# Keys of even tiles in the second place of the key buffer, and the first loads in another order

## The chip, the cores and the metric

The kernel runs on one core of one Trainium2 chip. The metric is the device time of one execution in microseconds (us). Engines: TensorE (PE, and PEld for its weight loads), VectorE (DVE), ScalarE (ACT), GpSimd (POOL), and SyncE (SP), which here only issues transfers.

## The reference, cut to what matters

The input is x of 4 batches x 1024 positions x 512. It goes through a layer norm, an attention with 16 heads of width 128, and a small product with quantised weights; all is added to x. Of the attention, these lines carry what the change touches:

```python
q  = apply_rope(rmsnorm(xn @ Wq + bq, qn_w), pos)
lk = apply_rope(rmsnorm(xn @ Wlk + blk, kn_w), pos)       # local keys
lv = xn @ Wlv + blv                                       # local values
sc = einsum(q, ck) * scale            # 256 compressed keys a batch, causal; the best 8 are kept
kw = concat([prev window of lk, this window of lk])       # windows of 128; none before the first
sl = where(band & (position exists), einsum(q, kw) * scale, NEG)
out = ((softmax(top 8) @ cv + softmax(sl) @ vw) * 0.5) @ Wo + bo
```

A query tile of 128 positions looks at its own 128 keys, at the 128 keys of the tile before it in the same batch, and at the compressed keys that are already complete. The first tile of a batch has no tile before it.

## The kernel before, in words

The work is cut into 256 units u = 64 * batch + 8 * pair + i: a pair of heads and a tile i of 128 positions. Unit u with u % 8 == 0 is the first tile of its batch for its pair of heads; there are 32 such units. The tiles of one pair follow each other, i = 0 to 7, so that the keys of the tile before are still in SBUF.

Every engine runs the same list of steps s, and in step s it works on several units at different stages: unit s is projected (`proj_qk`, lines 514 to 516), s-1 is transposed (`tr`, 540) and its values projected (`proj_v`, 530 to 532), s-2 is scored (`scores`, 561 to 563), s-3 has its weights transposed (`turn_p`, 571), s-4 meets the values (`values`, 586 and 589), s-5 goes through Wo (`out_proj`, 601 to 603). The order on each engine is written out by hand; engines wait for each other by semaphores. TensorE's order in a step is: first half of `proj_qk`, `scores`, `values`, second half of `proj_qk`, `tr`, `out_proj`, `turn_p`, `proj_v`.

Products that need more than the short float's precision are made of high and low halves in fp32r, three matmuls for one product. In `scores` these are q_hi by k_hi, q_hi by k_lo and q_lo by k_hi, for each of the two heads: six matmuls for a unit. The profile prints fp32r operands of matmuls as f32. Matmuls of plain f32 operands that are no transposes (`values`, and `entries` at line 631) appear as two records for one matmul in the code: `values` issues 384 matmuls at line 586, and the profile has 768.

The scored columns lie side by side in `qkh` and `qkl`, tiles of 5 x 128 columns for a head: 0 holds the queries, 1 and 2 hold local keys, 3 and 4 the compressed keys. Even tiles put their keys in place 1, odd tiles in place 2 (`qk_of`), so the other place still holds the tile before. `scores` takes n = 256 + C columns from place 1 on, with C = `width(u)` = 32 * (i + 1): 288 columns for a first tile, 512 for i = 7. A first tile uses only the 128 columns of its own keys (`nloc`) and the 32 compressed ones; place 2 is scored with it and not read. For the very first unit GpSimd fills place 2 with zeros (lines 1355 and 1356), and TensorE waits for that (semaphore `old`).

VectorE then adds a mask and takes the maximum (`mask_max`, 969), reading columns 0 to nloc of the scores; the block order of the weights in P follows the places, and `units_of` gives `values` the same order.

Before step 0 there are nine steps, from FIRST = -9 on, in which the eight tiles of batch 0 are normalised, transposed and split: VectorE `norm_stats` (1045 to 1049), GpSimd's power (1248), VectorE `normalise` (1056, 1060), TensorE `turn_x` (613) and `logits` (624), ScalarE `diagonal`, `hi_x`, `cast_x` (813, 791, 798), VectorE `group_max` and `lo_x` (1075, 1068). At the same time GpSimd splits the first weights (1303, 1305). In its order the split of chunk 0 stands ahead of the power of tile 1.

The first transfers stand in two queues. SP issues acc 0, acc 1, acc 2 (tiles of x), then chunks 0 and 1 of the weights, acc 3 and the rest. ACT issues `bcm`, `wcb`, `cst` (identity, masks, selectors: 352 KB) and two scalars into `isc`. VectorE waits for all of bcm, wcb and cst ahead of `normalise` of tile 0; TensorE waits for the same three before its first transpose.

Of the kernel before, what the change touches and what calls it, by code (L numbers as in the profile page):

```python
# [19 lines left out]
GONE = -3e38  # L20
# [5 lines left out]
C_ID, C_MK, C_MG, C_SEL, C_M32, C_N = 0, 128, 512, 640, 672, 704  # L26
# [4 lines left out]
FIRST, LAST = -AHEAD, NU + 6  # L31
# [9 lines left out]
    "kscale hi_qk p sq el es put_v hi_c wohi hi_x b8 ew put_et css hi_ck c8 "  # L41
    "lo_qk rs raw t1 krest add ngr mc m8 ttr mr nm lo_c acc wolo bs ba xv xn wl dg lo_x "
    "eg re wm init nb cke cm crest cadd cks lo_ck bl rsc isc wk tab rs0 "
# [4 lines left out]
).split()  # L48


def units_of(u):
    return [u] if u % 8 == 0 else [u, u - 1] if u % 2 == 0 else [u - 1, u]


def width(u):
    return 32 * (u % 8 + 1)


def nloc(u):
    return 128 if u % 8 == 0 else 256  # L60


def pblocks(u):
# [81 lines left out]
def build(nc, x, Wq, bq, Wcmp, bcmp, Wk, bk, Wv, bv, Wlk, blk, Wlv, blv, qnw, knw, Wo, bo,  # L145
# [3 lines left out]
    def sb(name, shape, dt=F32):  # L149
        return ctx.enter_context(nc.sbuf_tensor(name, shape, dt))  # L150
# [4 lines left out]
    with ctx:  # L155
        S = {name: ctx.enter_context(nc.semaphore("s_" + name)) for name in SIGNALS}
# [13 lines left out]
        qkh = sb("qkh", [128, 2, 5, 128], F32R)  # L170
        qkl = sb("qkl", [128, 2, 5, 128], F32R)
# [3 lines left out]
        t2 = sb("t2", [128, 2, 2, 64])  # L175
# [5 lines left out]
        P = sb("P", [128, 2, 2, 512])  # L181
        es = sb("es", [128, 2, 2, 256])
        rp = sb("rp", [128, 2, 256])
        e8 = sb("e8", [128, 2, 2, 8])
# [8 lines left out]
        q8 = sb("q8", [128, QR, 512], BF16)  # L193
# [3 lines left out]
        qb = sb("qb", [128, 512], BF16)  # L197
        qn = sb("qn", [128, 512], BF16)
# [6 lines left out]
        wcb = sb("wcb", [128, 512])  # L205
        bob = sb("bob", [128, 512])
        br = sb("br", [128, 2, 2, 2, 128])
        cst = sb("cst", [128, C_N])
# [16 lines left out]
        r4 = sb("r4", [128, 4, 4])  # L225
# [7 lines left out]
        bcm = sb("bcm", [128, 1])  # L233
# [6 lines left out]
        bS = [bS2[:, 0], bS2[:, 1]]  # L240
# [11 lines left out]
        def f32(ap):  # L252
            return ap.bitcast(F32)
# [14 lines left out]
        def bc(ap, n):  # L268
            return ap.rearrange("(a n) -> a n", a=1).broadcast_to([128, n])

        def qk_of(w, u):

            p = u % 2 + 1
            return w[:, :, 0:p + 1:p, :]

        def logits_of(t):
# [5 lines left out]
            return blT[:, n:n + 1]  # L282

        def mask_of(u):
            a = C_MK + 128 * (u % 2)
            return cst[:, a:a + nloc(u)]

        def w_halves(gi, c):
# [25 lines left out]
        def run_sync(e):  # L314
            def load_chunk(q):
                kind, gi, c, _ = CHUNKS[q]
                g = gi % NG
                if q >= 2:
                    k2, g2, c2, _ = CHUNKS[q - 2]
                    if k2 == "o":  # L320
                        e.wait_ge(S["wolo"], o_index(g2, c2) + 1)
                    else:
                        e.wait_ge(S["split"], w_index(g2, c2) + 1)
                dst, landed = wr[:, q % 2, :], S["d_w%d" % (q % 2)]
                if kind == "o":
                    h = 2 * g + c
                    e.dma_start(dst, Wo[h * 128:(h + 1) * 128, :]).then_inc(landed, 16)
                elif c < 4:
                    d4 = dst.rearrange("p (h k d) -> p h k d", h=2, k=2)
                    for j, w in enumerate((Wq, Wlk)):  # L330
                        src = w[c * 128:(c + 1) * 128, g * 256:(g + 1) * 256].rearrange("p (h d) -> p h d", h=2)
                        e.dma_start(d4[:, :, j, :], src).then_inc(landed, 16)
                else:
                    k0 = 2 * (c - 4)
                    src = Wlv[k0 * 128:(k0 + 2) * 128, g * 256:(g + 1) * 256].rearrange("(k p) n -> p k n", p=128)
                    e.dma_start(dst.rearrange("p (k n) -> p k n", k=2), src).then_inc(landed, 16)
# [39 lines left out]
            def load_acc(t):  # L376
                i = t % 8
                if t < 8:
                    e.dma_start(acc[:, i, :], x[0, i * 128:(i + 1) * 128, :]).then_inc(S["d_a%d" % i], 16)
                    return  # L380
                e.wait_ge(S["d_is"], 16 * (t - 7))
                e.wait_ge(S["d_o%d" % i], 16 * (t // 8))
                e.dma_start(acc[:, i, :], inis[t]).then_inc(S["d_a%d" % i], 16)
# [38 lines left out]

            load_acc(0)
            load_acc(1)
            load_acc(2)
            load_chunk(0)
            load_chunk(1)
# [25 lines left out]
            for s in range(FIRST, LAST):  # L453
# [26 lines left out]
                t = ffn_at(s, 5)  # L480
                if t is not None and t >= 8:
                    park_ini(t)
                t = tile_at(s + 1, "stats")
# [9 lines left out]
        def run_tensor(e):  # L493
# [50 lines left out]
            def scores(u, h):  # L544
                b, i, C = u // 64, u % 8, width(u)
                if h == 0:
                    e.wait_ge(S["lo_qk"], u + 1)
                    if u == 0:
                        e.wait_ge(S["old"], 1)
                        e.wait_ge(S["eg"], FIRST_TILES)  # L550
                    if b == 0 and i % 4 == 0:
                        e.wait_ge(S["lo_ck"], i // 4 + 1)
                    if i % 4 == 0 and b:
                        e.wait_ge(S["newck"], 2 * b - 1 + i // 4)
                if u >= 1:
                    e.wait_ge(S["es"], 2 * (u - 1) + h + 1)
                n = 256 + C
                q_, ql_ = qkh[:, h, 0, :], qkl[:, h, 0, :]
                kh = qkh[:, h, 1:5, :].rearrange("p a c -> p (a c)")[:, 0:n]
                kl = qkl[:, h, 1:5, :].rearrange("p a c -> p (a c)")[:, 0:n]  # L560
                e.matmul(bS[h][:, 0:n], q_, kh, start=True, stop=False)  # L561
                e.matmul(bS[h][:, 0:n], q_, kl, start=False, stop=False)  # L562
                e.matmul(bS[h][:, 0:n], ql_, kh, start=False, stop=True).then_inc(S["s"], 1)  # L563

            def turn_p(u, h):
                a = 2 * u + h
# [92 lines left out]
                last.then_inc(S["ff"], 1)  # L659
                free["Y"] = ("init", ffn_pos(t) + 1)  # L660

            e.wait_ge(S["d_c"], 16 * 3)
            for s in range(FIRST, 0):
                if tile_at(s, "turn") is not None:
                    turn_x(tile_at(s, "turn"))
# [42 lines left out]
        def run_scalar(e):  # L708
# [99 lines left out]

            def diagonal(t):
                e.wait_ge(S["wl"], t + 1)  # L810
                if t >= 1:
                    e.wait_ge(S["bc"], t)
                e.activation(dg[:, :], ident, ACT.Copy, scale=smt[:, t % 2, 2:3]).then_inc(S["dg"], 1)
# [37 lines left out]
                    dst, src = ckh[:, c], bT[:, 0:128]  # L851
                e.activation(dst, src, ACT.Copy).then_inc(S["hi_ck"], 1)

            e.dma_start(bcm[:, :], bc(bcmp, 1)).then_inc(S["d_c"], 16)
            e.dma_start(wcb[:, :], Wcmp.rearrange("n a -> a n").broadcast_to([128, 512])).then_inc(S["d_c"], 16)
            e.dma_start(cst[:, :], consts).then_inc(S["d_c"], 16)
            e.dma_start(isc[:, 0:1], bc(sc0, 1)).then_inc(S["d_s"], 16)
            e.dma_start(isc[:, 1:2], bc(sc1, 1)).then_inc(S["d_s"], 16)
            e.wait_ge(S["ones"], 1)
# [57 lines left out]
        def run_vector(e):  # L917
# [47 lines left out]
            def mask_max(u, h):  # L965
                e.wait_ge(S["s"], 2 * u + h + 1)
                if u >= 2:
                    e.wait_ge(S["pt"], 2 * (u - 2) + h + 1)
                e.tensor_tensor_reduce(P[:, u % 2, h, 0:nloc(u)], bS[h][:, 0:nloc(u)], mask_of(u), 1.0, GONE,  # L969
                                       ALU.add, ALU.max, mm[:, u % 4, h, 8:9]).then_inc(S["ttr"], 1)  # L970

            def max8(u, h):
# [176 lines left out]
            for s in range(FIRST, 0):  # L1149
                if tile_at(s, "stats") is not None:  # L1150
                    norm_stats(tile_at(s, "stats"))
                if s == FIRST + 2:
                    e.wait_ge(S["d_s"], 16 * 2)
                    e.tensor_scalar(isc[:, 2:4], isc[:, 0:2], 0.5, None, ALU.mult, ALU.bypass)
                    e.reciprocal(sm[:, 14:16], isc[:, 0:2]).then_inc(S["rsc"], 1)
                    e.wait_ge(S["rsc"], 1)
                    e.tensor_tensor(isc[:, 4:5], sm[:, 14:15], sm[:, 15:16], ALU.mult).then_inc(S["isc"], 1)
                if s == FIRST + 1:
                    e.wait_ge(S["d_c"], 16 * 3)
                if s == FIRST + 4:  # L1160
                    e.wait_ge(S["d_kv"], 16 * 4)
                    e.tensor_scalar(bkv[:, :], bkv[:, :], -1.0, None, ALU.mult, ALU.bypass).then_inc(S["nb"], 1)
                if tile_at(s, "wm") is not None:
                    weights4(tile_at(s, "wm"))
                if tile_at(s, "norm") is not None:
                    normalise(tile_at(s, "norm"))
                if tile_at(s, "max") is not None:
                    group_max(tile_at(s, "max"))
                    lo_x(tile_at(s, "lo"))
                if block_at(s, "rope") is not None:  # L1170
                    rope_ck(block_at(s, "rope"))
# [65 lines left out]
        def run_gpsimd(e):  # L1237
# [114 lines left out]
                                    ALU.mult)  # L1352
                e.tensor_tensor(wqk[:, :], wrow[:, 64:128], wrow[:, 192:256], ALU.mult).then_inc(S["tab"], 1)

            e.memset(f32(qkh[:, :, 2, :]), 0.0)
            e.memset(f32(qkl[:, :, 2, :]), 0.0).then_inc(S["old"], 1)
            e.memset(minus1[:, :], -1.0)
            e.memset(sq[:, :, 128:129], RMS_EPS)
            e.memset(mh[:, :], -0.5).then_inc(S["ones"], 1)
# [111 lines left out]
```

## Time and profile before

| | |
|---|---|
| median of 3 runs | 2570.6 us (2570.27 to 2572.04) |
| the profiled execution's own time | 2572.98 us |
| its span in the trace | 2571.2 us |
| TensorE busy, of the span | 98% |
| VectorE, ScalarE, GpSimd busy | 77%, 64%, 61% |
| granted TensorE clock, mean | 0.998 |

"Busy" is time with at least one instruction under way. Matmuls are pipelined: the time that one shows, from its start to its modelled end, is longer than the time until the next one starts, and what a matmul costs a queue that never stands still is that distance from start to start.

### The profile page before, as it was taken

The page shows a single profiled execution, that of the slowest core. Times are in us where ns is not written, and L with a number is a line of the kernel's source. Part 1 is how long each engine was busy: PE and PEld are TensorE (multiplying, and loading weights), DVE is VectorE, ACT ScalarE, POOL GpSimd, SP SyncE. Part 2 cuts the span into 40 slices and gives each one's busy share as a digit, 9 for nine tenths or more (in the row PEclk, how much of TensorE's full clock was granted, in tenths as well). Part 3 has the DMA queues.
Part 4 walks back from the last instruction along what each step waited for, and adds up shares of the span by engine and source line. Part 5 has one row for each costly group of instructions (what it writes and reads, how often), then busy time and mean ns, then how long its engine had stood idle before and what let it go on. Part 6 is the DMA issues. An engine that isn't in the chain of part 4 may idle for free. (4 is left out here: it accounts for less than half of the span.)

```text
span 2571.2 us, 54972 instructions
## 1 busy us (share of the span) xinstructions
PE 2525.6 (98%) x15288; PEld 2223.4 (86%) x15320; DVE 1985.2 (77%) x6309; ACT 1655.2 (64%) x4674; POOL 1569.2 (61%) x2768
## 2 busy tenths in 40 slices
PE   7999999999999999999999999999999999999998
PEld 5878888888888888888888888888888888888887
DVE  6888888888877778777877777877877776676775
ACT  4666666566666666666666666666666666666665
POOL 5777777776676555555556655555556655555554
PEclk9999999999999999999999999999999999999999
DMA  3531333223332212022243122121243221122101
GB/s 108 169 101 62 106 103 108 91 71 131 116 132 87 81 61 91 30 97 81 80 147 120 42 87 87 59 87 62 68 132 120 83 71 63 38 71 70 61 11 50
DMA packets 168291, 220.74 MB, mean 86 GB/s; under 512 B 17842, under 2 KB 89012, under 8 KB 167988
## 3 DMA queue, kind: packets, MB, share of 16 engines
q1 hardware_dynamic: 167268, 216.60, 25.7%
q8 instruction: 126, 2.06, 0.3%
q14 instruction: 177, 1.45, 0.2%
q10 hardware_dynamic: 720, 0.62, 0.1%
HBM read 156.35 MB, written 60.82 MB: 84 GB/s over the span
## 5 line engine op out<-in xcount | busy, mean ns | idle before, releaser
L1290 POOL TENSOR_TENSOR t<-raw,tB 128x128 f32<-128x128 f32 x512 | 227.9, 467 | 594.1 <-DVE raw L924 593.6
L1244 POOL TENSOR_TENSOR r<-ss,mh 128x4 f32<-128x4 f32 x256 | 286.8, 1120 | 261.2 <-DVE ss L941 261.2
L774 ACT ACTIVATE ch<-bVC,blT 128x128 fp32r<-128x128 f32 x512 | 160.3, 364 | 438.3 <-PE bVC L589 437.5
L514 PE MATMUL bQK<-wh,xh 128*128 128x512 f32 x1024 | 428.5, 418 | 0.8 <-DVE raw L924 0.8
L515 PE MATMUL bQK<-wl,xh 128*128 128x512 f32 x1024 | 405.4, 396 | 0.0
L516 PE MATMUL bQK<-wh,xl 128*128 128x512 f32 x1024 | 403.9, 394 | 0.0
L969 DVE CUSTOM_DVE_ANT_0 P<-bS,cst 128x256 f32<-128x256 f32 (+1 forms) x512 | 203.8, 398 | 159.4 <-PE bS L563 158.8
L530 PE MATMUL bVC<-wh,xh 128*128 128x256 f32 x1024 | 310.4, 303 | 4.9 <-DVE cl L1018 4.9
L741 ACT ACTIVATE P<-P,nm,r 128x256 f32<-128x256 f32 (+1 forms) x512 | 296.1, 586 | 0.0
L735 ACT ACTIVATE raw<-raw,r 128x128 f32<-128x128 f32 x512 | 178.4, 396 | 176.8 <-POOL r L1244 172.0
L532 PE MATMUL bVC<-wh,xl 128*128 128x256 f32 x1024 | 289.0, 282 | 0.0
L531 PE MATMUL bVC<-wl,xh 128*128 128x256 f32 x1024 | 288.8, 282 | 0.0
L1018 DVE SCALAR_TENSOR_TENSOR cl<-bVC,blT,ch 128x128 fp32r<-128x128 f32 x512 | 155.7, 346 | 169.8 <-ACT ch L774 169.0
L1279 POOL TENSOR_SCALAR P<-P,rs 128x256 f32<-128x256 f32 (+1 forms) x512 | 258.7, 505 | 19.6 <-POOL P L1266 11.0
L951 DVE TENSOR_TENSOR qkl<-bT,qkh 128x512 fp32r<-128x512 f32 x256 | 177.2, 692 | 116.2 <-ACT qkh L713 115.7
L589 PEld LDWEIGHTS bVC<-pt,v 128*128 128x128 f32 x1920 | 254.4, 191 | 13.4
L589 PE MATMUL bVC<-pt,v 128*128 128x128 f32 x1920 | 255.5, 275 | 0.0
L721 ACT ACTIVATE pt<-bP 128x512 f32<-128x512 f32 (+2 forms) x512 | 240.5, 525 | 2.5 <-PE bP L571 2.4
L571 PEld LDWEIGHTS bP<-cst,P 128*128 128x128 f32 x1728 | 204.6, 141 | 36.2 <-POOL P L1280 1.3
L516 PEld LDWEIGHTS bQK<-wh,xl 128*128 128x128 f32 x1024 | 193.6, 189 | 45.2
L571 PE MATMUL bP<-cst,P 128*128 128x128 f32 x1728 | 231.4, 273 | 0.3 <-POOL P L1280 0.2
L601 PE MATMUL bY<-woh,ch 128*128 128x512 f32 x512 | 224.2, 438 | 6.3 <-DVE ini L1119 4.8
(146 smaller groups left out, 6960.3 us busy)
## 6 DMA issues: line engine op xcount, KB each, us to landing
wh<-kept SPq DMA_DIRECT2D x144, 256.0 KB, 4.0
wl<-kept SPq DMA_DIRECT2D x144, 256.0 KB, 4.5
kept<-wh SPq DMA_DIRECT2D x48, 256.0 KB, 3.1
kept<-wl SPq DMA_DIRECT2D x48, 256.0 KB, 3.4
woh<-kepto SPq DMA_DIRECT2D x48, 256.0 KB, 3.4
wol<-kepto SPq DMA_DIRECT2D x48, 256.0 KB, 4.0
out<-acc SPq DMA_DIRECT2D x32, 256.0 KB, 3.1
ini<-in_hidden_states SPq DMA_DIRECT2D x24, 256.0 KB, 4.2
```

The lines of the kernel that those rows point to most:

```text
L514: e.matmul(bQK[:, :], a, b, start=kt == 0, stop=False)
L515: e.matmul(bQK[:, :], a, bl, start=False, stop=False)
L516: last = e.matmul(bQK[:, :], al, b, start=False, stop=kt == 3)
L530: e.matmul(bVC[:, 0:256], a, b, start=kt == 0, stop=False)
L531: e.matmul(bVC[:, 0:256], a, bl, start=False, stop=False)
L532: last = e.matmul(bVC[:, 0:256], al, b, start=False, stop=kt == KT - 1)
L571: last = e.transpose(bP[h][:, n * 128:(n + 1) * 128], P[:, u % 2, h, k * 128:(k + 1) * 128], ident)
L589: last = e.matmul(dst, v_[:, t % 4, h, :], pt[:, h, n * 128:(n + 1) * 128], start=False, stop=n == len(ts_) - 1 and h == 1)
L721: e.activation(pt[:, h, 0:n], bP[h][:, 0:n], ACT.Copy).then_inc(S["p"], 1)
L741: e.activation(pl, pl, ACT.Exp, scale=r4[:, u % 4, 2 * h:2 * h + 1], bias=nm[:, u % 4, h, 1:2], accum_out=su[:, u % 4, h, 1:2]).then_inc(S ...
L1244: e.tensor_tensor(r4[:, u % 4], ss[:, u % 4], mh[:, 0:4], ALU.pow).then_inc(S["r4"], 1)
L1279: e.tensor_scalar(pl, pl, rs[:, u % 4, h, 1:2], 0.5, ALU.mult, ALU.mult)
```

## The change

Keys of even tiles go to place 2 and those of odd tiles to place 1 (`qk_of`, `mask_of`, `units_of`). Then a first tile's keys stand right in front of the compressed keys, and its six score matmuls take columns 128 to 288: 160 in place of 288. All other units score as many columns as before, the two key places exchanged. The zeros in place 2 and the wait for them go. Beside it: `cst` is issued by SP, behind acc 1 and ahead of acc 2, with a semaphore of its own; on ACT `wcb` comes ahead of `bcm`; VectorE waits for these two ahead of tile 0's `normalise` and for `cst` one step later; it prepares the scalars of `isc` one step earlier; ScalarE's first `diagonal` waits for `cst`.

```diff
 def units_of(u):
-    return [u] if u % 8 == 0 else [u, u - 1] if u % 2 == 0 else [u - 1, u]
+    return [u] if u % 8 == 0 else [u - 1, u] if u % 2 == 0 else [u, u - 1]
+def first_key(u):
+    return 128 if u % 8 == 0 else 0
...
-            p = u % 2 + 1
+            p = 2 - u % 2
             return w[:, :, 0:p + 1:p, :]
...
-            a = C_MK + 128 * (u % 2)
+            a = C_MK + 128 * (u % 8 > 0 and u % 2 == 0)
             return cst[:, a:a + nloc(u)]
...
             load_acc(0)
             load_acc(1)
+            e.dma_start(cst[:, :], consts).then_inc(S["d_c"], 16)
             load_acc(2)
...
-                        e.wait_ge(S["old"], 1)
...
-                n = 256 + C
+                a, b_ = first_key(u), 256 + C
...
-                e.matmul(bS[h][:, 0:n], q_, kh, start=True, stop=False)
-                e.matmul(bS[h][:, 0:n], q_, kl, start=False, stop=False)
-                e.matmul(bS[h][:, 0:n], ql_, kh, start=False, stop=True).then_inc(S["s"], 1)
+                e.matmul(bS[h][:, a:b_], q_, kh, start=True, stop=False)
+                e.matmul(bS[h][:, a:b_], q_, kl, start=False, stop=False)
+                e.matmul(bS[h][:, a:b_], ql_, kh, start=False, stop=True).then_inc(S["s"], 1)
...
-            e.wait_ge(S["d_c"], 16 * 3)
+            e.wait_ge(S["d_c"], 16)
...
+                if t == 0:
+                    e.wait_ge(S["d_c"], 16)
...
-            e.dma_start(bcm[:, :], bc(bcmp, 1)).then_inc(S["d_c"], 16)
-            e.dma_start(wcb[:, :], Wcmp.rearrange("n a -> a n").broadcast_to([128, 512])).then_inc(S["d_c"], 16)
-            e.dma_start(cst[:, :], consts).then_inc(S["d_c"], 16)
+            e.dma_start(wcb[:, :], Wcmp.rearrange("n a -> a n").broadcast_to([128, 512])).then_inc(S["d_g"], 16)
+            e.dma_start(bcm[:, :], bc(bcmp, 1)).then_inc(S["d_g"], 16)
...
-                e.tensor_tensor_reduce(P[:, u % 2, h, 0:nloc(u)], bS[h][:, 0:nloc(u)], mask_of(u), 1.0, GONE,
+                e.tensor_tensor_reduce(P[:, u % 2, h, 0:nloc(u)], bS[h][:, first_key(u):256], mask_of(u), 1.0, GONE,
...
-                if s == FIRST + 2:
+                if s == FIRST + 1:
                     e.wait_ge(S["d_s"], 16 * 2)
...
                 if s == FIRST + 1:
-                    e.wait_ge(S["d_c"], 16 * 3)
+                    e.wait_ge(S["d_g"], 16 * 2)
+                if s == FIRST + 2:
+                    e.wait_ge(S["d_c"], 16)
...
-            e.memset(f32(qkh[:, :, 2, :]), 0.0)
-            e.memset(f32(qkl[:, :, 2, :]), 0.0).then_inc(S["old"], 1)
```

## Rows read from the trace of the kernel before

**Rows 1.** The page: busy time of each engine over the span.

```profile
PE 2525.6 (98%) x15288; PEld 2223.4 (86%) x15320; DVE 1985.2 (77%) x6309; ACT 1655.2 (64%) x4674; POOL 1569.2 (61%) x2768
```

**Rows 2.** Windows: all steps but the start and the end.

```profile
60.00:2540.00 2480.00, 2460.60 (x15002) 2169.60 (x15033) 1933.89 (x6155) 1613.63 (x4561) 1528.18 (x2703) 1.00 0.26 86
```

**Rows 3.** Waits of PE after 640 us, three windows: total, times, longest (us).

```profile
PE bT L540 <- DVE xsl L1068: 2.2, 1, 2.2
...
PE bY L601 <- DVE ini L1119: 0.7, 1, 0.7
...
PE bY L601 <- DVE ini L1119: 0.6, 1, 0.6
...
PE bVC L586 <- ACT pt L721: 2.0, 1, 2.0
```

**Rows 4.** Groups of matmuls by shape: tiles, moving shape, count, busy us, mean ns.

```profile
L530 PE MATMUL bVC<-wh,xh 128*128 128x256 f32 x1024 | 310.4, 303 | 4.9 <-DVE cl L1018 4.9
...
L586 PE MATMUL bVC<-pt,cv 128*128 128x256 f32 x768 | 210.4, 383 | 3.0 <-ACT pt L721 2.8
...
L561 PE MATMUL bS<-qkh 128*128 128x288 f32 x64 | 19.1, 298 | 0.0
L563 PE MATMUL bS<-qkh,qkl 128*128 128x288 f32 x64 | 18.9, 295 | 0.0
L562 PE MATMUL bS<-qkl,qkh 128*128 128x288 f32 x64 | 18.8, 294 | 0.0
```

**Rows 5.** Timeline of PE, a first tile's scores: start us, us, engine, line.

```profile
1259.59 0.29 PE L561 MATMUL bS<-qkh 128*128 128x288 f32 x1
...
1260.25 0.30 PE L563 MATMUL bS<-qkh,qkl 128*128 128x288 f32 x1
1260.38 1.03 PE L586 MATMUL bVC<-pt,cv 128*128 128x256 f32 x4
1261.24 0.94 PE L589 MATMUL bVC<-pt,v 128*128 128x128 f32 x7
```

**Rows 6.** Timeline of PE, the step before: 512 columns, then 32.

```profile
1248.65 0.39 PE L561 MATMUL bS<-qkh 128*128 128x512 f32 x1
...
1250.02 0.97 PE L631 MATMUL bY<-wm,xt 128*128 128x32 f32 x8
1250.83 1.11 PE L586 MATMUL bVC<-pt,cv 128*128 128x256 f32 x4
1251.78 0.61 PE L589 MATMUL bVC<-pt,v 128*128 128x128 f32 x4
```

**Rows 7.** Timeline of PEld, the weight loads of the same stretches.

```profile
1252.56 0.19 PEld L514 LDWEIGHTS bQK<-wh,xh 128*128 128x128 f32 x1
1252.67 0.19 PEld L515 LDWEIGHTS bQK<-wl,xh 128*128 128x128 f32 x1
...
1259.60 0.19 PEld L562 LDWEIGHTS bS<-qkl,qkh 128*128 128x128 f32 x1
1259.72 0.19 PEld L563 LDWEIGHTS bS<-qkh,qkl 128*128 128x128 f32 x1
```

**Rows 8.** Lines 561 and 563: duration, first and last start; who waited.

```profile
L561 PE MATMUL bS<-qkh x512: 292/347/476, 63.8 to 2550.0; 128*128 128x320 f32 x22, 128*128 128x416 f32 x22, 128*128 128x512 f32 x22, 128*128 128x288 f32 x21
...
  DVE P L969: 158.8, 149
```

**Rows 9.** Timeline of the first 13 us: zeros, loads, and who waits.

```profile
0.73 0.31 POOL L1355 MEMSET qkh<- 128x256 f32 x1 [0.29 <-POOLq L1456]
...
1.66 0.45 ACTq L856 DMA_DIRECT2D cst<-in_consts  x1
2.12 0.44 SPq L332 DMA_DIRECT2D wr<-in_Wq  x1
...
5.46 0.58 POOL L1248 TENSOR_TENSOR st<-st,mh 128x1 f32<-128x1 f32 x1 [3.94 <-DVE st L1049]
...
8.70 0.55 DVE L1056 TENSOR_SCALAR xt<-acc,st 128x512 f32<-128x512 f32 x1 [0.87 <-DMA cst<-in_consts]
...
9.83 0.69 POOL L1303 TENSOR_SCALAR wh<-wr 128x512 fp32r<-128x512 f32 x1 [3.79 <-DMA wr<-in_Wlk]
...
10.60 1.26 POOL L1305 TENSOR_TENSOR wl<-wr,wh 128x512 fp32r<-128x512 f32 x1
...
10.97 0.92 DVE L1154 TENSOR_SCALAR isc<-isc 128x2 f32<-128x2 f32 x1
...
11.82 0.56 POOL L1248 TENSOR_TENSOR st<-st,mh 128x1 f32<-128x1 f32 x1
...
11.98 0.16 DVE L1157 TENSOR_TENSOR isc<-sm 128x1 f32<-128x1 f32 x1
...
12.42 0.84 DVE L1056 TENSOR_SCALAR xt<-acc,st 128x512 f32<-128x512 f32 x1 [0.27 <-POOL st L1248]
```

More of the change, by code:

```diff
@@ L556, in scores @@
                     e.wait_ge(S["es"], 2 * (u - 1) + h + 1)
-                n = 256 + C
+                a, b_ = first_key(u), 256 + C
                 q_, ql_ = qkh[:, h, 0, :], qkl[:, h, 0, :]
-                kh = qkh[:, h, 1:5, :].rearrange("p a c -> p (a c)")[:, 0:n]
-                kl = qkl[:, h, 1:5, :].rearrange("p a c -> p (a c)")[:, 0:n]
-                e.matmul(bS[h][:, 0:n], q_, kh, start=True, stop=False)
-                e.matmul(bS[h][:, 0:n], q_, kl, start=False, stop=False)
-                e.matmul(bS[h][:, 0:n], ql_, kh, start=False, stop=True).then_inc(S["s"], 1)
+                kh = qkh[:, h, 1:5, :].rearrange("p a c -> p (a c)")[:, a:b_]
+                kl = qkl[:, h, 1:5, :].rearrange("p a c -> p (a c)")[:, a:b_]
+                e.matmul(bS[h][:, a:b_], q_, kh, start=True, stop=False)
+                e.matmul(bS[h][:, a:b_], q_, kl, start=False, stop=False)
+                e.matmul(bS[h][:, a:b_], ql_, kh, start=False, stop=True).then_inc(S["s"], 1)
             def turn_p(u, h):
```

4 rows, old and new, of the table SIGNALS are left out of this document.

## The prediction, as it stood before the run

> **What bounds the kernel now.** I read the busy line first. TensorE is busy 98% of the span, VectorE 77% [rows 1]. From the windows I take the stretch of all regular steps: 2460.6 of 2480 us busy, so TensorE stands still for 19.4 us in it, with a granted clock of 1.00, the 2.4 GHz level [rows 2]. The list of waits says where: after 640 us, where 24 of the 32 first tiles lie, TensorE waited for others 5.5 us in all, four times [rows 3]. So TensorE's own list of work is the bound, and what an instruction costs there is the distance from its start to the next start, not the 0.29 us that its row shows: six of 0.29 us would be 1.74 us, but the six of one first tile lie in 0.79 us. What is taken out of this list shortens the run almost by itself; what is taken from other engines does not.
>
> **The part on the main path: 192 matmuls of 160 columns.** A first tile has six score matmuls, and 32 first tiles make 192; the groups by shape show 64 for each of the three lines at 288 columns [rows 4]. Each is now 160 columns wide.
>
> Their price today: the six start at 1259.59 and the next work at 1260.38, 0.79 us, so 132 ns for one [rows 5]. Six of 512 columns take from 1248.65 to 1250.02, 1.37 us, 228 ns for one [rows 6]. Between the two sizes lie 224 columns and 96 ns: 0.43 ns a column. By this line alone one of 160 columns would cost 132 - 128 x 0.43 = 77 ns.
>
> But each matmul here brings a weight load of its own, and the number of loads stays. The row with almost nothing to stream shows what a load costs: eight records with 32 moving columns start at 1250.02, and the next work at 1250.83, 0.81 us. The four records behind them take 0.95 us (1250.83 to 1251.78), where the same four take 0.86 us one step later (1260.38 to 1261.24): 0.09 us of the loads is charged to them [rows 5, 6]. So 0.90 us for eight, 112 ns for one, though 32 columns need only a fraction of that to stream. The trace has the same figure for loads of an fp32r matmul: where short matmuls run ahead of them, the loads of lines 514 and 515 start 0.11 us apart, 1252.56 and 1252.67. In the score matmuls of 288 columns the loads start 0.12 us apart, paced by the matmuls [rows 7]. I read this as a floor: a matmul with its own load can't follow in less than 112 ns. 77 ns lies under it, so I take 112 ns for 160 columns.
>
> The sum: 6 x 112 = 0.67 us in place of 0.79 us, 0.12 us a first tile, and 32 x 0.12 = 3.8 us. The bounds of this price, since no fp32r matmul of the trace is narrower than 256 columns [rows 4]: below, 77 ns, which gives 55 x 192 = 10.6 us; above, the price of plain f32. There two records make a matmul, and a record of 256 columns takes 0.86 / 4 = 215 ns [rows 5], 0.84 ns a column, 1.68 for the pair: 160 columns would cost 269 ns, 137 more than today, and 192 x 137 = 26.3 us would be added. Between them I choose by the nearest rows: fp32r of 256 columns still goes by the 0.43 line (the unit's twelve matmuls of `proj_v` are in the same list at a mean of 303, 80 less than the 383 of plain f32 at that width), and the load floor is measured on both operand kinds.
>
> The Trainium skill says otherwise of the floor: "TensorE: Matmul & The Clock Gate", section "Back-to-back issue gap", gives a sustained spacing of about 81 ns for a stream of load and matmul pairs at 128 columns, and N/2.4 + 2.5 ns for a matmul seen alone. By the first, 160 columns would cost little more than 81 ns and the change would bring up to some 9.8 us; that is an estimate from the page. The trace doesn't agree: its loads are 112 ns apart even where the matmuls stream 32 columns [rows 6].
>
> **The same part on the other engines.** VectorE reads the same number of score columns for a first tile, at another offset. In all other units two places of equal size are exchanged: the same shapes, masks of the same width, the same four value tiles in another order. That is no instruction more and none longer, so it costs nothing even where nothing hides it. VectorE, which waits for scores 158.8 us in all [rows 8], gets a first tile's 0.12 us sooner.
>
> **The start.** The two memsets of 0.31 us go; GpSimd then idles 3.94 us until 5.46 [rows 9], so they are hidden, worth 0. The first score starts at 63.8 us [rows 8], so the wait for `old` is worth 0. `cst` was issued at 1.66 on ACT and is now third on SP, at about the same time. VectorE began tile 0's `normalise` at 8.70, having waited 0.87 us for cst; now only wcb, bcm and the scalars must be there. That can start tile 0 up to 0.87 us sooner, less the three small scalar instructions that now come ahead of it. What is late next is tile 1: its `normalise` starts at 12.42 and waits for GpSimd's power at 11.82, which stands behind the split of weight chunk 0, 9.83 to 11.82, and that split waited 3.79 us for its weights to land [rows 9]. So the gain on tile 0 stops there. Moving cst puts one issue of 0.45 us ahead of the weights' issue at 2.12 on SP's queue, with acc 2 and all behind it; the bytes ahead of them on both queues together stay the same. If the landing is bound by bytes, nothing moves; if by its issue, chunk 0 lands 0.45 us later and everything up to step 0 with it. The moved scalar work (three instructions at 10.97 to 12.14) was hidden beside that same wait. I take 0 for the start, with -0.5 and +0.5 as ends.
>
> **Sum.** Against the profiled execution: span 2571.2 - 3.8 = 2567.4, own time 2572.98 - 3.8 = 2569.2. That execution lies 2.4 us over the median of the runs, 2570.6; against the median the forecast is 2566.8 us, 0.15% less. A difference within 0.2%, 5.1 us, counts as none.
>
> **Rivals.**
> - *The load floor does not hold for fp32r* (the load of the next matmul overlaps more). For it: the floor under fp32r is seen at one pair of loads only. Against: those loads last as long as the others, 0.19 us, and are 0.11 us apart. Then 77 ns and -10.6 us: 2560.0. Chance 0.13.
> - *A narrow fp32r matmul loses its fast rate* and goes at the plain price, 269 ns. For it: the kernel has no fp32r matmul under 256 columns, so nothing here shows that the rate holds below; plain f32 is four times dearer a column, so there is something to lose. Against: from 512 to 256 columns nothing bends. Then +26.3 us: 2596.9, slower. It decides from 132 + 5140 / 192 = 159 ns a matmul on. Chance 0.14. [...]
> - *It streams at half rate but in one pass*, as a record of plain f32 does: 160 x 0.84 = 134 ns, and the shorter matmul costs what the longer did: 2570.6 + 0.4 = 2571.0, no change. Chance 0.06.
> - *The start moves by more than I allow*: the weights land late and the delay grows over tiles. 1 us more would cancel a quarter of the gain, no class changes. Chance 0.03.
>
> **How the numbers follow.** The forecast has 0.64. Within it the result crosses 5.1 us if the floor is nearer 107 than 112 ns (6 x 25 x 32 = 4.8 us) and the start gives its 0.5: one in six of it. Faster: 0.13 + 0.11 = 0.24. Slower: 0.14 and 0.03 for what I don't see: 0.17. Within 0.2%: 0.59. The range reaches from the first rival, 2560.0, to the half-rate one with 1 us of a late start and the spread of single runs, 2573.0; outside it lie the plain price and a little more, under 2 in 10. The likeliest case alone: 2565.5 to 2568.0.
>
> **What would show it.** In the trace after, lines 561 to 563 have 64 records each of 128x160, and six of them with the next start take about 0.67 us (0.46 us under the first rival, 1.6 us under the second, 0.8 us under the third); weight loads of these lines lie 0.11 us apart. The steps of all other tiles keep their length. Tile 0's `normalise` starts before 8.70, tile 1's near 12.4, and the first step begins where it did, within half a microsecond. The prediction is wrong if the six take over 0.96 us or under 0.6, or if TensorE, sooner done, waits in the step of a first tile for something that I took for hidden.

## The result: 3.8 us less, and the profile after

The changed kernel took 2567.85 us in the median of 21 runs (2566.49 to 2570.70), the kernel before 2571.64 us in the median of 21 (2568.86 to 2574.95). The ratio is 0.9986 with a 95% interval of 0.9981 to 0.9992: 0.14% less, within the 0.2% that count as none, and clear of zero. The forecast was 0.15% less. In microseconds the interval reaches from 2.1 to 4.9 us less.

The profiled execution took 2566.60 us, its span is 2564.8 us. That is 6.4 us less than the span of the profiled execution before, more than the medians differ. The page shows TensorE still at 98%:

```profile
span 2564.8 us, 54971 instructions
PE 2515.7 (98%) x15288; PEld 2216.1 (86%) x15320; DVE 1984.2 (77%) x6309; ACT 1652.2 (64%) x4674; POOL 1565.7 (61%) x2766
```

The count of matmuls and of weight loads is that of [rows 1]; GpSimd has two instructions less, the memsets. Next the groups of the score matmuls by shape. The 64 records of each line have 160 columns, and their mean is 19 to 39 ns under the 294 to 298 of [rows 4], less than the 55 ns that 128 columns fewer would save at 0.43 ns each. That is only a hint, since a record's duration is not its price:

```profile
L568 PE MATMUL bS<-qkh,qkl 128*128 128x160 f32 x64 | 17.6, 275 | 0.0
L567 PE MATMUL bS<-qkl,qkh 128*128 128x160 f32 x64 | 17.6, 275 | 0.0
L566 PE MATMUL bS<-qkh 128*128 128x160 f32 x64 | 16.6, 259 | 0.0
```

What they cost the queue is seen in the timeline. It is the same first tile as in [rows 5]:

```profile
1255.28 0.23 PE L566 MATMUL bS<-qkh 128*128 128x160 f32 x1
1255.35 0.28 PE L567 MATMUL bS<-qkl,qkh 128*128 128x160 f32 x1
1255.46 0.28 PE L568 MATMUL bS<-qkh,qkl 128*128 128x160 f32 x1
1255.57 0.28 PE L566 MATMUL bS<-qkh 128*128 128x160 f32 x1
1255.68 0.27 PE L567 MATMUL bS<-qkl,qkh 128*128 128x160 f32 x1
1255.79 0.28 PE L568 MATMUL bS<-qkh,qkl 128*128 128x160 f32 x1
1255.91 1.06 PE L591 MATMUL bVC<-pt,cv 128*128 128x256 f32 x4
1256.81 0.61 PE L594 MATMUL bVC<-pt,v 128*128 128x128 f32 x4
```

From the second on they start 0.11 us apart. Six take 0.63 us (1255.28 to 1255.91), and the four records behind them 0.90 us in place of 0.86, so 0.04 us of the six is charged there: 0.67 us, as forecast, against 0.79. The weight loads of these lines keep the same distance:

```profile
1255.28 0.19 PEld L567 LDWEIGHTS bS<-qkl,qkh 128*128 128x128 f32 x1
1255.39 0.19 PEld L568 LDWEIGHTS bS<-qkh,qkl 128*128 128x128 f32 x1
1255.50 0.19 PEld L566 LDWEIGHTS bS<-qkh 128*128 128x128 f32 x1
1255.61 0.19 PEld L567 LDWEIGHTS bS<-qkl,qkh 128*128 128x128 f32 x1
1255.72 0.19 PEld L568 LDWEIGHTS bS<-qkh,qkl 128*128 128x128 f32 x1
```

Step by step, from TensorE's first record of one step to that of the next, both traces give the same length, within 0.06 us, for every regular step from step 66 on, with one exception: the steps in which a first tile is scored are 0.127 us shorter in the median. From the start of step 64 to that of step 255 lie 1842.64 us before and 1839.61 after, 3.03 us less for the 24 first tiles in between, 0.126 each. For 32 that makes 4.0 us.

**The other 2.4 us between the two profiled executions arise in the first 13 steps, and the moments at which TensorE's clock rises are enough to make them: the kernel before shows the same course against itself (experiment 2).** Before, TensorE is at half rate until 61 us; this is its timeline there, with the starts 0.42 us apart for 512 columns, the 1.2 GHz level:

```profile
58.62 0.63 PE L514 MATMUL bQK<-wh,xh 128*128 128x512 f32 x1
59.04 0.63 PE L515 MATMUL bQK<-wl,xh 128*128 128x512 f32 x1
```

The profile's own value for the clock does not show this. The first change that it recorded in this execution is at 61 us, and for the stretch before it gives 1.00 (the third number from the right), so here the rate is read from the distances:

```profile
48.00:60.00 12.00, 10.66 (x31) 8.18 (x31) 4.33 (x11) 2.83 (x9) 4.55 (x6) 1.00 0.07 20
```

In the profiled execution after, TensorE has its full rate once from 37.3 to 44.1 us, falls back, and has it again from 51 us on; the same matmuls of the same step start 0.24 us apart:

```profile
56.01 0.40 PE L520 MATMUL bQK<-wh,xh 128*128 128x512 f32 x1
56.25 0.39 PE L521 MATMUL bQK<-wl,xh 128*128 128x512 f32 x1
```

At the start of step 2 the execution after is 3.8 us ahead (58.56 and 62.39). It loses 2.3 us of that in step 7, where TensorE waits 1.81 us for VectorE in place of 0.46 and, after only, the granted clock is at half from 112.4 to 115.8 us. At the start of step 13 it is 2.5 us ahead (170.18 and 172.66). The experiments show that these moments move from execution to execution of the same kernel.

In the first 13 us the new order of loads does something too. The timeline of VectorE and GpSimd after:

```profile
5.49 0.69 DVE L1051 BATCH_NORM_STATS2 st<-acc 128x6 f32<-128x512 f32 x1 [5.49 <-DMA acc<-in_hidden_states]
...
9.18 0.17 DVE L1160 TENSOR_SCALAR isc<-isc 128x2 f32<-128x2 f32 x1 [1.58 <-DMA isc<-in_scale]
...
9.54 0.55 DVE L1062 TENSOR_SCALAR xt<-acc,st 128x512 f32<-128x512 f32 x1
9.89 0.67 POOL L1311 TENSOR_SCALAR wh<-wr 128x512 fp32r<-128x512 f32 x1 [2.58 <-DMA wr<-in_Wlk]
...
12.86 0.77 DVE L1062 TENSOR_SCALAR xt<-acc,st 128x512 f32<-128x512 f32 x1 [0.74 <-POOL st L1256]
```

Tile 0's `normalise` starts at 9.54, where it started at 8.70 [rows 9]: it now waits for the scalars of `isc`, which landed at 9.18. Weight chunk 0 landed as before (9.89 against 9.83), and tile 1's `normalise` starts at 12.86, 0.44 us later.

### The profile page after: what moved, and what is told of

Read it like the earlier page. It is cut to its first block and busy times, and to the rows that moved or that the text cites. A ratio compares the mean times of both kernels' runs of the same rounds, so it can differ in the third digit from the quotient of the medians.

```text
span 2564.8 us, 54971 instructions
## 1 busy us (share of the span) xinstructions
PE 2515.7 (98%) x15288; PEld 2216.1 (86%) x15320; DVE 1984.2 (77%) x6309; ACT 1652.2 (64%) x4674; POOL 1565.7 (61%) x2766
## 5 line engine op out<-in xcount | busy, mean ns | idle before, releaser
L957 DVE TENSOR_TENSOR qkl<-bT,qkh 128x512 fp32r<-128x512 f32 x256 | 177.1, 692 | 115.8 <-ACT qkh L718 115.3
```

## The experiments

The theory on record is the load floor: a matmul that brings its own weight load takes at least 112 ns, so 160 columns save 0.12 us a first tile and no more, all of it reaches the end, and the new order of loads is worth nothing. Each experiment was run beside the kernel before on the same chip.

**1. The changed kernel again, and its two parts alone.** Three kernels, the first the unchanged text of the changed kernel.

> The changed kernel once more, as the yardstick for the three others on this chip. Theory L (load floor: a narrow matmul costs its weight load, 112 ns): 3.8 to 4.0 us less than the kernel before. Theory S (a rival: most of the gain of 6.4 us between the two profiled executions is in the first 100 us and belongs to the reordered loads): also less, by 4 to 6 us. It also gives one more sample of the moment at which the granted clock rises in the first steps.

The key places alone, the start as before:

```diff
             load_acc(1)
-            e.dma_start(cst[:, :], consts).then_inc(S["d_c"], 16)
             load_acc(2)
...
-                if s == FIRST + 1:
+                if s == FIRST + 2:
                     e.wait_ge(S["d_s"], 16 * 2)
```

with bcm, wcb and cst on ACT's queue and the waits as before.

> The key places and the 160 columns alone, the first loads as in the kernel before. Theory L: the whole gain stays, 3.8 to 4.0 us under the kernel before, and within 0.5 us of the changed kernel. Theory S: less than half of it stays, under 2 us.

The start alone: the kernel before with the lines of the diff that deal with cst, wcb, bcm and isc.

> The kernel before with the new order of the first loads and waits alone; 288 columns as before. Theory L: no gain, within 0.5 us of the kernel before. Theory S: 2 us or more under it.

| kernel | median us (lowest to highest, runs) | ratio to before, 95% interval |
|---|---|---|
| kernel before, same chip | 2571.66 (2568.74 to 2575.02, 33) | |
| changed kernel again | 2567.45 (2566.52 to 2570.39, 11) | 0.9987 (0.9978 to 0.9996) |
| key places alone | 2568.21 (2566.18 to 2570.72, 11) | 0.9988 (0.9979 to 0.9996) |
| start alone | 2573.92 (2572.14 to 2575.70, 11) | 1.0009 (1.0000 to 1.0018) |

The key places alone carry the gain, 3.5 us; the rival that gave it to the start falls. But the start alone lay 2.3 us above the kernel before, which the theory had not expected. Its trace: steps 64 to 255 take 1842.63 us, as before (1842.64), and 1.6 us stand in the tail, where nothing of the start is left: from the start of step 255 to the end it is 40.16 us in place of 38.55. This is the granted clock there, in the windows of that trace (the third number from the right):

```profile
2557.00:2560.40 3.40, 3.40 (x13) 3.04 (x13) 0.00 (x0) 0.47 (x2) 1.34 (x3) 0.50 0.21 80
```

and TensorE's timeline just before it: a wait of 2.04 us for ScalarE, then the four records of line 587 in 1.46 us, which took 0.97 in the trace of before:

```profile
2556.51 1.67 PE L587 MATMUL bVC<-pt,cv 128*128 128x256 f32 x4 [2.04 <-ACT pt L722]
2557.97 1.92 PE L590 MATMUL bVC<-pt,v 128*128 128x128 f32 x8
```

The same wait of 2.04 us is in the trace of before, and there the four records behind it ran at their usual distance. That explains this one execution; what the ten others spent their time on no trace shows.

**2. The same three again, with the kernel before as a fourth,** to tell the clock's chance from a real cost of the start.

> The kernel before, run as if it were a new one, beside itself: it shows how far two equal kernels lie apart here. No difference is expected; 1 us apart would still be chance, as single runs spread over 6 us. In its trace the granted clock may rise and dip at other moments than in the first trace.

> The new order of the first loads alone, again. Its first measurement lay 2.3 us above the kernel before, and 1.6 us of the difference in its trace stood in the last steps, where the granted clock was at half, far from the loads. Theory C (chance of the clock): this time within 1 us of the kernel before. Rival (the new order costs something real): 2 us above it again.

> Key places and 160 columns alone, again: 4.0 us under the kernel before by the sum over 32 first tiles of 0.127 us. If the new order of loads costs 2 us by itself, this kernel must lie 2 us under the changed one; if not, beside it.

> The changed kernel a third time, on the same chip as these three: 3.5 to 4.5 us under the kernel before, and within 1 us of the kernel with the key places alone.

| kernel | median us (lowest to highest, runs) | ratio to before, 95% interval |
|---|---|---|
| kernel before, same chip | 2572.10 (2568.79 to 2575.16, 33) | |
| kernel before as a new one | 2571.75 (2569.68 to 2572.99, 11) | 0.9999 (0.9990 to 1.0007) |
| start alone | 2571.94 (2569.51 to 2574.34, 11) | 1.0001 (0.9992 to 1.0010) |
| key places alone | 2567.99 (2565.60 to 2570.91, 11) | 0.9988 (0.9979 to 0.9997) |
| changed kernel, third time | 2568.40 (2565.47 to 2572.12, 11) | 0.9987 (0.9979 to 0.9996) |

The 2.3 us did not come back, and the tail of this trace is 38.55 us again. Over both measurements the start alone lies 1 us above the kernel before, with the two at 2.3 above and 0.2 below; a cost or gain under 1 us is not settled by this. One of 2 us is made unlikely by the pair of changed kernel and key places alone, which differ by -0.8 and +0.4 us.

The traces of the two unchanged kernels give the size of the clock's chance. The kernel before, profiled twice, has spans of 2571.2 and 2567.9 us; steps 64 to 255 take 1842.64 and 1842.89 us, and the 3.3 us lie in the start and the first 64 steps: TensorE's half rate of the first steps ends at 61 us in the one and at 50 us in the other. The second is 4.5 us ahead of the first at step 2, 2.1 at step 8 and 3.1 at step 13, the course that the changed kernel has against the first. The changed kernel, profiled three times, has spans of 2564.8, 2565.5 and 2563.6 us with 1839.61, 1839.62 and 1839.54 us for steps 64 to 255. The start alone has 1842.63 and 1842.60 us there, the key places alone 1839.96 and 1839.81, so the 3 us belong to the key places and their narrower matmuls. So a comparison of this stretch resolves 0.3 us from single traces, where the whole time needs many runs.

**3. Far fewer columns.**

```diff
-                a, b_ = first_key(u), 256 + C
+                a, b_ = (256 if u % 8 == 0 and u >= 64 else first_key(u)), 256 + C
```

> The changed kernel, but from batch 1 on a first tile scores only its 32 compressed columns; the 128 local scores of these 24 first tiles are left out (what VectorE reads there is stale). Theory L: 32 columns cost as much as 160, 112 ns, so the time is that of the changed kernel within 0.5 us. Rival (the price follows the columns down, 0.43 ns each): 6 x 24 x 128 x 0.43 ns = 7.9 us less than the changed kernel.

This kernel leaves out the local scores of 24 first tiles. Measured: 2568.03 us (2566.34 to 2570.66, 11 runs), ratio 0.9989 (0.9980 to 0.9998); the changed kernel beside it had 2567.45. Steps 64 to 255 take 1839.48 us. The timeline of a first tile, 32 columns each:

```profile
1256.63 0.18 PE L566 MATMUL bS<-qkh 128*128 128x32 f32 x1
1256.66 0.26 PE L567 MATMUL bS<-qkl,qkh 128*128 128x32 f32 x1
1256.77 0.26 PE L568 MATMUL bS<-qkh,qkl 128*128 128x32 f32 x1
1256.88 0.26 PE L566 MATMUL bS<-qkh 128*128 128x32 f32 x1
1257.00 0.26 PE L567 MATMUL bS<-qkl,qkh 128*128 128x32 f32 x1
1257.11 0.26 PE L568 MATMUL bS<-qkh,qkl 128*128 128x32 f32 x1
1257.22 1.11 PE L591 MATMUL bVC<-pt,cv 128*128 128x256 f32 x4
1258.17 1.06 PE L594 MATMUL bVC<-pt,v 128*128 128x128 f32 x8
```

0.59 us, and 0.09 charged to the four behind (0.95 us in place of 0.86): 0.68 us for six. A fifth of the columns costs the same. The rival of a price that follows the columns, 7.9 us less, falls.

**4. More columns than needed.**

```diff
-                a, b_ = first_key(u), 256 + C
+                a, b_ = (64 if u % 8 == 0 and u >= 64 else first_key(u)), 256 + C
```

> The changed kernel, but from batch 1 on a first tile scores 224 columns, the 64 nearest of place 1 with its own, which nobody reads. Where does the floor meet the line? Theory L: the line gives 105 ns for 224 columns, under the floor, so 112 ns and the time of the changed kernel within 0.5 us. Rival (no floor, the line from 160 columns up): 6 x 24 x 64 x 0.43 ns = 4.0 us more.

Measured: 2568.75 us (2565.89 to 2570.72, 10 runs) beside 2574.27 us (2570.63 to 2576.01, 13 runs) of the kernel before, ratio 0.9979 (0.9970 to 0.9988). The changed kernel was not run in this group, where the kernel before lay 2.6 us over its median of the first group, so the 5.5 us between these two medians are no measure against the changed kernel; the trace is. Steps 64 to 255 take 1839.90 us, 0.3 us more than in the changed kernel, which is what single traces resolve; without a floor it would be 4.0 us more. In the timeline 224 columns are as far apart as 160 and as 32:

```profile
1255.43 0.27 PE L568 MATMUL bS<-qkh,qkl 128*128 128x224 f32 x1
1255.55 0.28 PE L566 MATMUL bS<-qkh 128*128 128x224 f32 x1
1255.66 0.27 PE L567 MATMUL bS<-qkl,qkh 128*128 128x224 f32 x1
```

**5. The same columns with twice the loads.** Each matmul of a first tile is cut into two of 80 columns.

```diff
+                for lo in ((a, a + 80) if u % 8 == 0 else (a,)):
+                    hi = lo + 80 if u % 8 == 0 else b_
+                    o, kh_, kl_ = bS[h][:, lo:hi], kh[:, lo - a:hi - a], kl[:, lo - a:hi - a]
+                    e.matmul(o, q_, kh_, start=True, stop=False)
+                    e.matmul(o, q_, kl_, start=False, stop=False)
+                    last = e.matmul(o, ql_, kh_, start=False, stop=True)
+                last.then_inc(S["s"], 1)
```

> Each score matmul of a first tile cut into two of 80 columns: 12 matmuls and 12 weight loads for the same 960 columns. Theory L (each load costs 112 ns, the columns nothing beside it): 6 x 112 ns more a first tile, 0.67 x 32 = 21.5 us more than the changed kernel. Rival (columns set the price, at 0.43 ns and some 8 ns fixed): under 2 us more.

Measured: 2590.25 us (2587.52 to 2592.17, 4 runs), ratio 1.0064 (1.0049 to 1.0079); that is 21.5 us over the 2568.75 of experiment 4, which by its trace costs what the changed kernel does. In the trace, a step with a first tile is 0.55 us longer than in the kernel before, so 0.68 us longer than in the changed one: 6 x 112 ns. In the timeline all are 0.11 us apart from the second on, here the last two:

```profile
1268.87 0.28 PE L570 MATMUL bS<-qkl,qkh 128*128 128x80 f32 x1
1268.98 0.28 PE L571 MATMUL bS<-qkh,qkl 128*128 128x80 f32 x1
1269.09 1.11 PE L595 MATMUL bVC<-pt,cv 128*128 128x256 f32 x4
```

**6. The upper bound: plain f32.**

```diff
+                if u % 8 == 0:
+                    q_, ql_, kh, kl = f32(q_), f32(ql_), f32(kh), f32(kl)
```

> The six score matmuls of a first tile with their operands read as plain f32, 160 columns as in the changed kernel. It measures the upper bound of the prediction. By it: 269 ns a matmul in place of 112, 157 x 192 = 30.1 us more than the changed kernel, in two records of about 134 ns each. If a record of plain f32 under 256 columns were paced by something else than 0.84 ns a column: 112 ns a record would give 21.5 us more.

Measured: 2597.28 us (2593.67 to 2600.66, 4 runs), ratio 1.0092 (1.0077 to 1.0107), 28.5 us over experiment 4. A step with a first tile is 0.83 us longer than in the kernel before, 0.96 us longer than in the changed one, 30.7 us for 32. Each line now has two records for a matmul, and the matmuls start 0.27 us apart, 136 ns a record:

```profile
1266.10 0.43 PE L568 MATMUL bS<-qkh 128*128 128x160 f32 x2
1266.37 0.43 PE L569 MATMUL bS<-qkl,qkh 128*128 128x160 f32 x2
1266.64 0.43 PE L570 MATMUL bS<-qkh,qkl 128*128 128x160 f32 x2
```

So at 160 columns fp32r still goes in one record, at 112 ns, where plain f32 takes 272: the rate is not lost below 256 columns.

**7. A saving twenty times as large.**

```diff
-                a, b_ = first_key(u), 256 + C
+                a, b_ = (96 + C if u >= 64 else first_key(u)), 256 + C
```

> The changed kernel, but from batch 1 on every tile scores only 160 columns, the last ones; the rest of the scores of 168 units is left out (stale columns are read). It asks how much of a much larger saving on TensorE reaches the end. If TensorE stays the bound: from the distances in the trace, 0.21 to 0.70 us less for a tile i = 1 to 7, 3.2 us a pair and batch, 24 of them, 77 us less than the changed kernel. If another engine or a chain between engines takes over, clearly less than that, with new waits on TensorE.

Measured: 2494.74 us (2493.61 to 2495.83, 4 runs), ratio 0.9692 (0.9676 to 0.9708), 74.0 us under experiment 4. In the trace the steps are shorter by 0.22, 0.29, 0.40, 0.46, 0.55, 0.64 and 0.71 us for i = 1 to 7, in the median; 3.27 us for the seven, 78.5 for 24 sets. From the start of step 64 to that of step 255 it is 72.4 us less than in the changed kernel, where these medians alone would give 76.6; 4 us do not arrive. TensorE's waits from 700 us on are 6.2 us in all, of which the 2.1 us stand in the last steps, as in the kernel before [rows 3]:

```profile
PE bY L606 <- DVE ini L1125: 2.8, 2, 1.4
PE bVC L591 <- ACT pt L726: 2.1, 1, 2.1
PE bY L606 <- DMA wol<-kepto: 1.0, 1, 1.0
PE bVC L591 <- issue: 0.3, 1, 0.3
```

TensorE is still the bound with 3% less work. Some 95% of what is taken from its list arrives at the end.

## Why the prediction was right

**The bound.** Right: the regular steps have the same length in both traces but for those of the first tiles, and experiment 7 shows that 74.0 us of a saving that was put at 77 pass through.

**The price of 160 columns.** Right: 0.67 us for six, 112 ns each. The floor was read from rows with 32 columns of plain f32 [rows 6] and one pair of fp32r loads [rows 7]; experiments 3, 4 and 5 show it for fp32r at 32, 80, 160 and 224 columns, and that the number of matmuls, each with its load, sets the price. Whether the load itself or something else in each matmul makes the 112 ns is not separated: no run has fp32r matmuls without loads of their own, and experiment 5 doubles both. The prediction named the load; the sum is the same either way. The line over 288 and 512 columns, alone, would have promised 10.6 us. The floor is why 44% fewer columns took 15% off the price: 132 to 112 ns.

**The sum.** 3.8 us forecast, 4.0 us by the steps of the traces, 3.8 by the first medians, and 4.2 and 3.7 by the two later measurements of the changed kernel. That forecast and first medians agree to a tenth is luck, with an interval of 2.1 to 4.9 us. The time itself, 2567.85 us, lies 1.05 us over the forecast of 2566.8, since the kernel before has a median of 2571.64 in 21 runs and had 2570.6 in the three that the forecast started from.

**The rivals.** The floor that doesn't hold fell with experiment 3: 32 columns cost as much as 160. The Trainium skill's figure of about 81 ns for pairs of load and matmul at 128 columns ("TensorE: Matmul & The Clock Gate", "Back-to-back issue gap") belongs to it and is not met here, where they are 112 ns apart at 32 to 224 columns; for the load alone the same page's section "LDWEIGHTS (loading the stationary operand)" gives columns / 1.2 ns, an estimate of 107 ns, and the runs show loads 112 ns apart. The plain price fell with experiment 6, which measured it: 272 ns, where the prediction had 269. The half rate in one pass, 134 ns, fell with the trace after.

**The start.** The total was right, 0 within half a microsecond as far as the runs tell, but a step of it failed. "That can start tile 0 up to 0.87 us sooner": it started 0.84 us later. VectorE had done tile 0's and tile 1's statistics by 7.60 and then waited 1.58 us for the scalars, which now stand ahead of `normalise` and landed at 9.18; their three instructions follow, and `normalise` starts at 9.54. Tile 0's rows landed late too, at 5.49 in place of 4.20, but that was over before the scalars came. The prediction had counted the three scalar instructions and not their transfer's landing. All ten traces with the new order have TensorE's first transposes at 10.2 to 10.4 us, the four with the old order at 9.3 to 9.4; the next tile's follow at 16.3 to 16.4, against 15.9 to 16.0 in three of the four and 16.3 in one. This 0.4 us is tile 1's, as foreseen for a late landing, though the weights landed on time: GpSimd's split of chunk 0, 9.89 to 12.22, ran 0.3 us longer. That step 0 began between 38.1 and 40.8 us with the new order and between 37.8 and 40.5 with the old tells little, since it moves with the clock. Three traces can be compared: in them TensorE is at half rate up to 61 us, so all of the start goes at one rate. There step 0 begins at 40.8 with the new order, and at 40.3 and 40.5 with the old: 0.2 to 0.4 us later, inside the half microsecond that the prediction allowed. The medians can't resolve that.

**What the prediction left out** is the clock. It treated the difference between an execution's time and the median as given. The profiled pair differed by 6.4 us, and whoever took it for the effect would have been off by 2.4.

## What to carry to other kernels

On TensorE look at the distance of the weight loads before you narrow the moving operand: at 224 columns of fp32r and fewer a matmul with its load cost 112 ns here (119 at 256 columns), and there only fewer matmuls help, not fewer columns. A floor can be read from any row of the trace where almost nothing streams. For effects under 0.2% compare the same stretch of steps in two traces: here single traces agree to 0.3 us over 1840 us, while whole executions spread over 6 us.

## What the runs showed of the hardware that was not expected

- TensorE's half rate of the first steps (the 1.2 GHz level) ends between 50 and 61 us over the 14 traces, at 61 and at 50 us in the two of the kernel before. In eleven of them the full rate comes once before, between 34 and 37 us, and goes again between 42 and 45 us. This and short stretches at half clock later, some of them in places where the same wait passed without one in another trace, move the total: the two traces of the kernel before differ by 3.3 us. The later stretches follow waits of TensorE: in the trace of before, one from 139.7 us behind a wait of 1.81 us, one from 665.3 us behind one of 2.2 us. A stretch at half clock in the last steps cost 1.6 us (experiment 1); TensorE had stood still for 2.04 us before it.
- fp32r matmuls of 32 to 224 columns start 112 ns apart, those of 256 columns 119 (eleven of `proj_v` from 1252.58 to 1253.89 in the trace after; the line over 288 and 512 columns gives 118), those of 288 columns 132.
- Plain f32 at 160 columns takes two records of 136 ns, so its price follows the columns there, where fp32r's has stopped doing so.
